# One-hots for an edge selection written as 2-byte marks and widened on a second engine, with six tiles selected in two chunks of five

## The chip, the cores and the metric

The kernel runs on one core of a Trainium2 chip. The metric is the device time of one execution in microseconds (us). Before the change the runs shown have a median of 3418.08 us, and the execution that was profiled took 3413.38 us. A core has five engines that run their own instruction streams and meet at semaphores: TensorE (PE, matrix products), VectorE (DVE), ScalarE (ACT), GpSimd (POOL, here the engine that starts row gathers) and SyncE (SP, here a queue of plain DMAs).

## The reference

One graph-attention layer over 12500 nodes and 400000 edges, the edges sorted by destination:

```python
h = jnp.maximum(_layernorm(x, axis=-1), 0.0)
xl = jnp.einsum('ni,nio->no', h, hetero_w[node_type]) + hetero_b[node_type]
ete = _lrelu(edge_type_emb[edge_type])
eae = _lrelu(edge_attr @ edge_attr_w)
alpha = _lrelu(jnp.concatenate([xl[dst], xl[src], ete, eae], axis=-1) @ att_w)
amax = jax.ops.segment_max(alpha, dst, num_segments=N)
alpha = jnp.exp(alpha - amax[dst])
denom = jax.ops.segment_sum(alpha, dst, num_segments=N)
alpha = alpha / (denom[dst] + 1e-16)
msg = jnp.concatenate([xl[src], eae], axis=-1) @ lin_w * alpha
out = x + jax.ops.segment_sum(msg, dst, num_segments=N)
```

## The kernel before

A prologue builds a table with one row of 34 numbers for each node (its contribution to messages and its two attention scores) and stores it in DRAM. The edges then go by in 125 chunks. A chunk has 25 tiles of 128 edges, one edge of a tile on each partition. The loop body is five chunks long (`u` = 0 to 4, each with its own buffers) and runs 25 times; the last pass is written out for most engines.

For each edge the table row of its source node is needed. It comes in one of two ways. **20 of the 25 tiles are gathered**: POOL issues one indirect DMA per tile (`gather_chunk`, line 598), two chunks ahead. **Five tiles are selected** (`TS = 5`): DVE compares a broadcast list of codes with constants and so writes one-hot matrices in a 4-byte format (`select_onehots`, lines 1150 and 1152, seven compares for `sel_a`, the first three tiles, and seven for `sel_b`, the last two); PE multiplies them with the table, which lies in SBUF in seven groups and two parts (`select`, 14 products at line 834 and one at 836), into the one PSUM bank `ps_sel`; DVE takes the row out of the bank (`take`, line 1164). There is a single bank, so `select` number j waits for `take` number j-1 (`sel_read`), and `take` j waits for `select` j (`sel_mm`).

Everything else of a chunk: PE computes destination scores in seven steps (`dst_scores`, line 848, read by DVE in `picks`, line 1172), the edge attributes (`attr_product`, 858), messages (`messages`, 869) and sign counts (`count_signs`, 878). DVE adds gathered rows to the messages (line 1241), forms the scores and a running maximum, hands `args` to ACT (1263), and scans the weighted messages in two halves (`scan_half`, 1220). ACT takes the exponential (728), spreads it into `keep` (735), which the first scan waits for, copies the sums into rows (741), starts their store (744), and writes the sign matrices for the next chunk (`make_signs`, 718 and 720).

The order on each engine is written out by hand. DVE's pass for chunk c works on chunk c's sums and on the selection and scores of chunk c+1, whose products PE runs at the same time: `take` 0 stands after `select_rest` for c+1, `take` 1 between the two scans, `take` 2 behind the attribute activation, `select_first` (for c+2) behind that, and then `take` 3 and `take` 4. On PE the five `select`s of a chunk stand between the steps of `dst_scores`.

At the end a fix-up joins runs of edges that cross partitions: SP waits for all row stores and loads the last row of each partition back into `tails`, DVE and PE work on it, POOL gathers one row (`own`, 613) and scatters one (616). Then POOL gathers 98 blocks of rows for the nodes, in eight groups of 19, 17, 17 and five times 9 (`last_in_buf`, line 639), and DVE finishes each group when its gathers have landed (lines 1468 to 1480): marks of a node's last block in `is_node` and `is_last`, a product with them (1472), two reductions (1474, 1475), a reciprocal, a product and a sum, after which SP stores the group.

Of the kernel before, what the change touches and what calls it, by code (L numbers as in the profile page):

```python
# [14 lines left out]
P = 128  # L15
# [22 lines left out]
TS = 5  # L38
TS_A = 3
SEL = CHUNKS * TS  # L40
GATHERED = T - TS
TURNS = tuple(GATHERED * k // 5 for k in range(6))
# [24 lines left out]
def gnn_kernel(nc, x, meta, dst_rows, dst_tmajor, type_tmajor, sel_src, row_edges, row_last, edge_attr_t, node_type,  # L67
# [20 lines left out]
    with ctx:  # L88
# [99 lines left out]
        compared = node_buf[:, 2 * TG * P:2 * TG * P + (EPP + 1) // 2].bitcast(bf16)[:, 0:EPP]  # L188
        eae_s = in_node_buf(0, [2, TG * P // 2], G * F_EDGE)
        eae = in_node_buf(TG * P, [2, TG * P // 2], G * F_EDGE)  # L190
        dstc = [sb(f"dstc{u}", [P, T + 1]) for u in range(U)]
# [29 lines left out]
        def part_of(k, g):  # L221
            return parts[:, k, g, :].rearrange("p (f n) -> p f n", n=GN)

        last_in_buf = [(buf.rearrange("p (n j f) -> p n j f", j=BLOCK, f=RW), n) for buf, n in (
            *((b.bitcast(fp32)[:, 0:9 * BLOCK * RW], 9)
              for b in (*(buf[:] for buf in hib_sb), onehot[:].rearrange("p t e -> p (t e)"))),
# [3 lines left out]
        is_node = hm[0][:].rearrange("p a b -> p (a b)")[:, 0:NPP * (BLOCK + 1)].rearrange("p (n j) -> p n j", j=BLOCK + 1)  # L230
        is_last = hm[1][:].rearrange("p a b -> p (a b)")[:, 0:NPP * BLOCK].rearrange("p (n j) -> p n j", j=BLOCK)
# [16 lines left out]
        tails = sb("tails", [P, RW])  # L248
# [31 lines left out]
        ps_hmT = [ps_attr, ps_pick]  # L280

# [61 lines left out]
        eae_scaled = sem("eae_scaled")  # L343
        eae_ready = sem("eae_ready")
# [13 lines left out]
        tails_in = sem("tails_in")  # L358
# [31 lines left out]
        out_ready = sem("out_ready")  # L390
        out_done = sem("out_done")
# [6 lines left out]
        def selected(i, u):  # L398

            return (i * U + u) * TS  # L400
# [12 lines left out]
        def _(sp):  # L413
# [95 lines left out]

            for u in range(U):  # L510
                sp.wait_ge(stored[u], 16 * ITERS + 1)
            flag = is_unsorted(sp)
            sp.wait_ge(sel_mm, count(CHUNKS * TS))
            sp.dma_start(x_end[:], x).then_inc(x_end_in, 16)
            with sp.If(flag < 1):
                sp.dma_start(tails[:], rows_pm[:, EPP - 1, :]).then_inc(tails_in, 16)
                sp.wait_ge(tails_in, 16)
# [17 lines left out]
        def _(pool):  # L535
# [50 lines left out]
            def gather_chunk(i, u, first):  # L586
# [6 lines left out]
                for k, (phase, reached) in enumerate(phases):  # L593
                    if not first:
                        pool.wait_ge(phase, reached)
                        pool.sem_inc(gather_turns, 1)
                    for t in range(TURNS[k], TURNS[k + 1]):
                        nc.gpsimd.indirect_dma_start(  # L598
                            gath[u][:, t, :], None, table_dram,
                            bass.IndirectOffsetOnAxis(ap=meta_sb[u][:, t:t + 1], axis=0)).then_inc(gathered[u], 16)  # L600

            for u in range(U):
                gather_chunk(0, u, u < AHEAD)
            with pool.Fori(1, ITERS) as i:
                for u in range(U):
                    gather_chunk(i, u, False)

            for u in range(U):
                pool.wait_ge(stored[u], 16 * ITERS + 1)
            flag = is_unsorted(pool)  # L610
            with pool.If(flag < 1):
                pool.wait_ge(head_idx_ready, 1)
# [32 lines left out]
        def _(act):  # L645
            start_at_one(act, rows_sums, *stored)
# [65 lines left out]

            def make_signs(c, u):
# [10 lines left out]
            def chunk(i, u, final):  # L724
                c = i * U + u

                act.wait_ge(args_ready, c + 1)
# [16 lines left out]
                act.dma_start(rows_pm[:, ds(c * T, T), :], rows[u][:]).then_inc(stored[u], 16)  # L744
                if not final:
# [3 lines left out]
            make_signs(0, 0)  # L749
            with act.Fori(0, ITERS - 1) as i:  # L750
# [21 lines left out]
        def _(pe):  # L772
# [51 lines left out]
            def select(c, j):  # L824

                if j == 0:
                    pe.wait_ge(sel_a_ready, c + 1)
                elif j == TS_A:
                    pe.wait_ge(sel_b_ready, c + 1)
                rows_of, slots_of, at = (sel_a, slot_a, j) if j < TS_A else (sel_b, slot_b, j - TS_A)  # L830
                pe.wait_ge(sel_read, count(c * TS + j))
# [52 lines left out]
            with pe.Fori(0, ITERS) as i:  # L884
                for u in range(U):
                    c = i * U + u
                    dst_scores(c, 0)
                    select(c, 0)
                    attr_product(i, u)
                    dst_scores(c, 1)  # L890
                    select(c, 1)
                    dst_scores(c, 2)
                    dst_scores(c, 3)
                    select(c, 2)
                    dst_scores(c, 4)
                    messages(c)
                    select(c, 3)
                    dst_scores(c, 5)
                    dst_scores(c, 6)
                    select(c, 4)  # L900
                    count_signs(c)

            pe.wait_ge(falls_ready, 1)
            pe.wait_ge(sel_read, count(CHUNKS * TS))
            nc.tensor.matmul(ps_misc[:, 0, 0:1], before_me[:], falls[:, 0:1], start=True, stop=True).then_inc(
                falls_mm, 1)
# [7 lines left out]
            with pe.If(flag < 1):  # L914
                pe.wait_ge(tails_in, 16)
# [5 lines left out]
                nc.tensor.matmul(ps_misc[:, 0, 2 * P:2 * P + VW], wtailT[:], tails[:, 0:VW], start=True,  # L921
# [14 lines left out]
        def _(dve):  # L936
# [208 lines left out]
            def select_onehots(i, u, tiles, rows_of, slots_of, ready):  # L1145
# [3 lines left out]
                for g in range(NG):  # L1149
                    v.tensor_scalar(rows_of[:, g, :, 0:P], code_sb[u][:, edges], part_group[:, g:g + 1], None,  # L1150
                                    ALU.is_equal)
                v.tensor_scalar(slots_of[0:GN, :, 0:P], slot_sb[u][:, edges], part[0:GN, :], None,  # L1152
                                ALU.is_equal).then_inc(ready, 1)

            def select_first(i, u):
                select_onehots(i, u, slice(0, TS_A), sel_a, slot_a, sel_a_ready)

            def select_rest(i, u):
                select_onehots(i, u, slice(TS_A, TS), sel_b, slot_b, sel_b_ready)
# [65 lines left out]
            def chunk(i, u, at, final):  # L1225
# [4 lines left out]
                last_front = isinstance(i, int) and c + 2 >= CHUNKS  # L1230

# [5 lines left out]
                dve.wait_ge(gathered[u], (i + 1) * (16 * GATHERED))  # L1237
                dve.wait_ge(msg_mm, count(c + 1))
                dve.wait_ge(sel_read, count(selected(i, u) + TS))
# [4 lines left out]
                if not final:  # L1244
                    select_rest(*after)
# [31 lines left out]
                if not final:  # L1277
                    picks(front, 2)
                    attr_act(front)
                    take(*after, 2)  # L1280
                    picks(front, 3)
                    if not last_front:
                        select_first(*later)
                    picks(front, 4)
                    take(*after, 3)
# [5 lines left out]
                    take(*after, 4)  # L1291
# [4 lines left out]
            select_first(0, 0)  # L1296
# [14 lines left out]
            select_rest(0, 0)  # L1311
# [72 lines left out]


            flag = is_unsorted(dve)
            with dve.If(flag < 1):
                joined_step = stage(join_step)
                dve.wait_ge(tails_in, 16)
                v.tensor_copy(mtail[:], tails[:, VW:VW + 1].broadcast_to([P, P])).then_inc(head_idx_ready, 1)  # L1390
# [70 lines left out]
            finished = stage(last_step)  # L1461

            finished(v.memset(is_node, 0.0))
            dve.wait_ge(x_end_in, 16)
            for k, (buf, w) in enumerate(last_in_buf):
# [3 lines left out]
                                         node_id[:, n].unsqueeze(2).broadcast_to([P, w, BLOCK]), ALU.is_equal))  # L1469
                finished(v.tensor_tensor(is_last[:, n, :], is_node[:, n, 0:BLOCK], is_node[:, n, 1:BLOCK + 1],  # L1470
# [59 lines left out]
```

## Time and profile before

| | |
|---|---|
| median of the runs shown | 3418.08 us |
| the profiled execution | 3413.38 us |
| its span, first to last instruction | 3411.6 us |
| PE busy | 3067.4 us (90%) |
| DVE busy | 2951.0 us (86%) |
| POOL busy | 2495.9 us (73%) |
| ACT busy | 900.4 us (26%) |
| mean granted TensorE clock | 0.954 |

Busy shares are means over a prologue of some 150 us, the loop of about 3090 us and an end of some 170 us. POOL's share leaves out the fixed time between two DMA issues, which the profile counts as idle for "issue". Matmuls overlap, so the time from the start of one group to the start of the next says more than their durations; the same holds for short DVE instructions in a row.

### The profile page before, as it was taken

What the parts mean: (1) busy time and instruction counts of PE and PEld (TensorE: products, weight loads), DVE (VectorE), ACT (ScalarE), POOL (GpSimd) and SP (SyncE); (2) the same over time, 40 slices, a digit from 0 to 9 for tenths busy, and PEclk for the clock granted to TensorE, in tenths of its full rate; (3) what the DMA queues carried; (4) which work ended last, traced back from release to release, by engine and by line L of the source; (5) the groups of instructions that cost most, each with busy time, mean ns of one, the idle gap of its engine ahead of it and who ended that gap; (6) DMA issues with size and microseconds to landing.
All of it is one profiled execution on the core that took longest, in us unless ns stands there. A gap on an engine that the chain in (4) does not pass through costs nothing.

```text
span 3411.6 us, 66571 instructions
## 1 busy us (share of the span) xinstructions
PE 3067.4 (90%) x21488; PEld 2610.0 (77%) x21488; DVE 2951.0 (86%) x7241; ACT 900.4 (26%) x2094; POOL 2495.9 (73%) x2629
## 2 busy tenths in 40 slices
PE   7799999999999999999999999999999999999900
PEld 6688888878878888888888888888887887887700
DVE  6799999889889888988989889888988988998835
ACT  3223232223222232222323223232222222222200
POOL 2577777777777777777777777777777777777656
PEclk6799999999999999999999999999999999999955
DMA  3433333333333333333333333333333333336322
GB/s 119 117 73 91 72 91 72 91 72 86 77 72 91 72 88 76 79 85 72 91 72 83 80 72 91 72 88 78 76 89 72 91 72 73 91 72 153 74 74 73
DMA packets 186011, 284.37 MB, mean 83 GB/s; under 512 B 73954, under 2 KB 140986, under 8 KB 185212
## 3 DMA queue, kind: packets, MB, share of 16 engines
q1 hardware_dynamic: 76796, 165.55, 16.1%
q0 software_dynamic: 84768, 52.50, 13.0%
q10 hardware_dynamic: 24288, 64.79, 5.3%
q14 instruction: 131, 1.07, 0.1%
q8 instruction: 28, 0.46, 0.1%
HBM read 210.13 MB, written 72.48 MB: 83 GB/s over the span
## 4 chain that ended last, share of the span: by engine, by line
DVE 28%; PE 27%; POOL 23%; issue 17%; DMA 4%; DVEq 0%; POOLq 0%; ACT 0%; SPq 0%; ACTq 0%
POOL gath L598 20%; PE ps_misc L834 19%; DVE sel_a L1150 10%; DMA gath<-table_dram,meta 4%; DVE sel_b L1150 4%; DVE gath L1164 3%; PE ps_pick L848 3%; DVE dscore L1172 3%; DVE slot_a L1152 1%; PE ps_misc L836 1%; DVE ps_msg L1241 1%; PE ps_misc L804 1%; POOL hib L639 1%; DVE ps_misc L1211 1%; PE ps_attr L858 1%
## 5 line engine op out<-in xcount | busy, mean ns | idle before, releaser
L598 POOL DMA_INDIRECT gath<-table_dram,meta x2500 | 2364.3, 946 | 831.8 <-issue 733.3
L834 PE MATMUL ps_misc<-parts,sel_a 128*128 128x462 f32 x5250 | 1219.0, 383 | 94.3 <-DVE gath L1164 94.1
L834 PEld LDWEIGHTS ps_misc<-parts,sel_a 128*128 128x128 f32 x5250 | 973.9, 191 | 220.6 <-DVE gath L1164 120.4
L834 PE MATMUL ps_misc<-parts,sel_b 128*128 128x462 f32 x3500 | 806.5, 381 | 28.4 <-DVE gath L1164 25.0
L834 PEld LDWEIGHTS ps_misc<-parts,sel_b 128*128 128x128 f32 x3500 | 644.9, 189 | 117.8 <-DVE gath L1164 43.6
L848 PE MATMUL ps_pick<-s_dst,onehot 122*128 122x128 bf16 x9375 | 652.4, 220 | 29.6 <-DVE s_dst L1304 14.2
L848 PEld LDWEIGHTS ps_pick<-s_dst,onehot 122*128 122x128 bf16 x9375 | 540.0, 98 | 172.9 <-issue 126.2
L1172 DVE TENSOR_REDUCE dscore<-ps_pick 128x4 f32<-128x512 f32 x875 | 521.5, 618 | 1.2 <-PE ps_pick L848 1.1
L1164 DVE TENSOR_REDUCE gath<-ps_misc 128x33 f32<-128x462 f32 x625 | 391.9, 627 | 142.3 <-PE ps_misc L836 142.3
L728 ACT ACTIVATE wts<-args 128x50 f32<-128x50 f32 x125 | 30.8, 246 | 1680.5 <-DVE args L1263 1680.5
L1150 DVE TENSOR_SCALAR sel_a<-dst_f,part_group 128x384 fp32r<-128x384 f16 x875 | 465.4, 604 | 0.0
L741 ACT COPY rows<-sums 128x825 f32<-128x825 f32 x125 | 231.2, 1849 | 500.0 <-DVE sums L1220 500.0
L1220 DVE TENSOR_TENSOR_SCAN sums<-keep,ps_misc 128x416 f32<-128x416 f32 x250 | 261.9, 1048 | 9.3 <-ACT keep L735 0.3
L1150 DVE TENSOR_SCALAR sel_b<-dst_f,part_group 128x256 fp32r<-128x256 f16 x875 | 266.3, 375 | 0.0
L718 ACT ACTIVATE hi_f<-half,hic 128x128 bf16<-128x128 f32 x625 | 243.5, 390 | 82.3 <-ACT rows L741 77.1
L1185 DVE TENSOR_SCALAR onehot<-hib,row_code 122x3200 bf16<-122x3200 bf16 x125 | 232.1, 1857 | 0.0
L720 ACT ACTIVATE hi_f<-half,loc 128x98 bf16<-128x98 f32 x625 | 226.2, 362 | 0.0
L1241 DVE TENSOR_TENSOR ps_msg<-gath,ps_msg 128x495 f32<-128x495 f32 x250 | 135.8, 589 | 87.0 <-DMA gath<-table_dram,meta 86.4
L869 PE MATMUL ps_msg<-msg_w,node_buf 80*128 80x165 f32 x1250 | 202.4, 309 | 0.0
L869 PEld LDWEIGHTS ps_msg<-msg_w,node_buf 80*128 80x128 f32 x1250 | 177.7, 190 | 0.0
L1211 DVE TENSOR_TENSOR ps_misc<-ps_msg,wts 128x240 f32<-128x240 f32 x500 | 159.2, 364 | 0.2 <-ACT wts L728 0.2
L858 PE MATMUL ps_attr<-attr,attr_w 80*80 80x320 f32 x500 | 155.1, 432 | 0.0
(239 smaller groups left out, 1933.5 us busy)
## 6 DMA issues: line engine op xcount, KB each, us to landing
hib<-digit_dram SPq DMA_DIRECT2D x125, 612.5 KB
rows_dram<-rows ACTq DMA_DIRECT2D x125, 437.5 KB, 5.0
gath<-table_dram,meta POOLq DMA_INDIRECT x2500
attr<-edge_attr_t_in SPq DMA_DIRECT2D x125, 200.0 KB
dst_f<-sel_code_dram SPq DMA_DIRECT2D x125, 160.0 KB
hib<-digit_dram SPq DMA_DIRECT2D x250, 50.0 KB
rows_dram<-no_rows ACTq DMA_DIRECT2D x1, 8575.0 KB, 44.5
hib<-digit_dram SPq DMA_DIRECT2D x250, 25.0 KB
```

The source lines that it names most:

```text
L598: nc.gpsimd.indirect_dma_start(gath[u][:, t, :], None, table_dram, bass.IndirectOffsetOnAxis(ap=meta_sb[u][:, t:t + 1], axis=0)).then_inc( ...
L718: nc.scalar.activation(sign_hi[:, t, :], half128[:], ACT.Sign, bias=hic[u][:, t:t + 1], scale=-1.0)
L720: last = nc.scalar.activation(sign_lo[:, t, :], half128[:, 0:NPP], ACT.Sign, bias=loc[u][:, t:t + 1], scale=-1.0)
L741: nc.scalar.copy(rows[u][:, :, 0:VW], sums[:, :, 1:T + 1].rearrange("p f t -> p t f")).then_inc(rows_sums, 1)
L834: nc.tensor.matmul(ps_sel, rows_of[:, g, at, 0:P], parts[:, k, g, :], start=(g == 0 and k == 0), stop=False)
L848: last = nc.tensor.matmul(ps_pick[:, g % 2, j * LO:(j + 1) * LO], onehot[0:KD, t, 0:P], s_dst[0:KD, k, :], start=(k == 0), stop=(k == 2))
L869: last = nc.tensor.matmul(ps_msg[:, g // 3, g % 3 * G * VW:(g % 3 + 1) * G * VW], eae_flat[:, g * P:(g + 1) * P], msg_w[:], start=True, st ...
L1150: v.tensor_scalar(rows_of[:, g, :, 0:P], code_sb[u][:, edges], part_group[:, g:g + 1], None, ALU.is_equal)
L1164: v.tensor_reduce(gath[u][:, T - 1 - j, 0:VW], ps_sel.rearrange("p (f n) -> p f n", n=GN), AX.X, ALU.max).then_inc(sel_read, 1)
L1172: v.tensor_reduce(dscore[:, tiles], ps_pick[:, g % 2, 0:n * LO].rearrange("p (t m) -> p t m", m=LO), AX.X, ALU.max).then_inc(picked, 1)
L1185: v.tensor_scalar(onehot[0:KD, :, 0:P], hib_sb[HIB_OF[u]][0:KD, :], row_code[0:KD, :], None, ALU.is_equal).then_inc(onehot_ready, 1)
L1220: return v.tensor_tensor_scan(sums[:, f0:f1, :].rearrange("p f t -> p (f t)"), keep[:, f0:f1, :].rearrange("p f t -> p (f t)"), terms[:, 0 ...
```

## The change

The selection's one-hots are made in two steps. DVE's compares for chunks after the first now write contiguous bf16 marks into one shared buffer `marks` (`select_marks`, seven compares of 384 or 256 numbers), and ACT copies the marks, widened to the 4-byte format, into `sel_a` (`widen_first`, 7x384 numbers) and `sel_b` (`widen_rest`, 7x256 or 7x384). Two new semaphores order this: `marks_ready` (DVE to ACT) and `marks_widened` (ACT to PE, and to DVE before the buffer is written again). The small one-hots of slots stay with DVE.

The number of selected tiles follows `TS_OF = (5, 6, 5, 6, 5)`: chunks with `u` = 1 and 3 select six tiles and gather 19. A pass of the loop selects 27 tiles instead of 25 and gathers 98 instead of 100; over the kernel POOL issues 2450 gathers instead of 2500.

In the end, the last rows of the partitions are read where they still lie in SBUF (`row_tails`) and the load of `tails` is gone; POOL's gather of `own` no longer waits for DVE; clearing `is_node` is moved ahead; `is_last`, a copy of `node_id`, the reciprocals and the averages lie in PSUM; the last group of nine nodes is split in six and three; and `count_falls` and the load of `x_end` stand a little earlier.

```diff
-TS = 5
+TS_OF = (5, 6, 5, 6, 5)
+TS = max(TS_OF)
 TS_A = 3
-GATHERED = T - TS
-TURNS = tuple(GATHERED * k // 5 for k in range(6))
...
+            (hib_sb[0][:].bitcast(fp32)[:, 6 * BLOCK * RW:9 * BLOCK * RW], 3),
+            (hib_sb[0][:].bitcast(fp32)[:, 0:6 * BLOCK * RW], 6),
...
+        is_last = [in_bank(ps_msg, 0, BLOCK * last_at[k], w, BLOCK) for k, (_, w) in enumerate(last_in_buf)]
+        inverse = ps_msg[:, 1, 0:NPP]
+        node_of = ps_msg[:, 1, NPP:2 * NPP]
+        averaged = ps_pick[:].rearrange("p a b -> p (a b)")
+        row_tails = rows[U - 1][:, T - 1, :]
...
+            def widen_rest(i, u):
+                c = i * U + u
+                before = (i, u - 1) if u else (i - 1, U - 1)
+                n = TS_OF[u] - TS_A
+                act.wait_ge(marks_ready, 2 * c)
+                act.wait_ge(sel_mm, count(selected(*before) + TS_OF[before[1]]))
+                nc.scalar.copy(sel_b[:, :, 0:n, 0:P],
+                               marks[:, :, 0:n * P].rearrange("p g (t e) -> p g t e", e=P)).then_inc(marks_widened, 1)
...
+            def select_marks(i, u, tiles, widened):
+                edges = slice(tiles.start * P, tiles.stop * P)
+                dve.wait_ge(code_in[u], (i + 1) * 32)
+                dve.wait_ge(marks_widened, widened)
+                for g in range(NG):
+                    last = v.tensor_scalar(marks[:, g, 0:edges.stop - edges.start], code_sb[u][:, edges],
+                                           part_group[:, g:g + 1], None, ALU.is_equal)
+                last.then_inc(marks_ready, 1)
...
                 if not final:
                     picks(front, 2)
                     attr_act(front)
-                    take(*after, 2)
+                    if takes > 2:
+                        take(*after, 2)
                     picks(front, 3)
                     if not last_front:
                         select_first(*later)
+                    if takes > 5:
+                        take(*after, 3)
                     picks(front, 4)
-                    take(*after, 3)
+                    if takes > 3:
+                        take(*after, takes - 2)
```

On PE, in a chunk with `u` = 1, from its second `select` to the step after its third; before:

```order
L834 MATMUL ps_misc<-parts,sel_a 128x462 x14
L836 MATMUL ps_misc<-slot_pen,slot_a 128x462
L842 REGISTER_ALU
L848 MATMUL ps_pick<-s_dst,onehot 128x128 x12
L842 REGISTER_ALU
L848 MATMUL ps_pick<-s_dst,onehot 128x128 x12
L831 REGISTER_ALU
L834 MATMUL ps_misc<-parts,sel_a 128x462 x14
L836 MATMUL ps_misc<-slot_pen,slot_a 128x462
L842 REGISTER_ALU
L848 MATMUL ps_pick<-s_dst,onehot 128x128 x12
```

The same place now, on to the fourth `select`, which uses the first tile of `sel_b`:

```order
L884 MATMUL ps_misc<-parts,sel_a 128x462 x14
L886 MATMUL ps_misc<-slot_pen,slot_a 128x462
L892 REGISTER_ALU
L898 MATMUL ps_pick<-s_dst,onehot 128x128 x12
L881 REGISTER_ALU
L884 MATMUL ps_misc<-parts,sel_a 128x462 x14
L886 MATMUL ps_misc<-slot_pen,slot_a 128x462
L892 REGISTER_ALU
L898 MATMUL ps_pick<-s_dst,onehot 128x128 x12
L879 REGISTER_ALU
L881 REGISTER_ALU
L884 MATMUL ps_misc<-parts,sel_b 128x462 x14
```

Where two score steps stood between the second and the third `select`, one stands now, and one between the third and the fourth; chunks with five tiles keep the old order.

On ACT, one chunk from the exponential (728 before, 772 now) to the first sign matrix (718, 757); before:

```order
L728 ACTIVATE wts<-args 128x50
L731 COPY rows<-mrun 128x25
L732 COPY rows<-dstc 128x25
L735 COPY keep<-wts 128x33x25
L709 REGISTER_ALU
L711 ACTIVATE node_buf<-ps_attr 80x640
L741 COPY rows<-sums 128x25x33
L744 ISA
L744 DMA rows_dram<-rows 128x875
L718 ACTIVATE hi_f<-half,hic 128x128
```

And now, the two widening copies being the lines named CAST:

```order
L749 CAST sel_b<-node_buf 128x7x2x128
L772 ACTIVATE wts<-args 128x50
L775 COPY rows<-mrun 128x25
L776 COPY rows<-dstc 128x25
L779 COPY keep<-wts 128x33x25
L729 REGISTER_ALU
L731 ACTIVATE node_buf<-ps_attr 80x640
L785 COPY rows<-sums 128x25x33
...
L739 CAST sel_a<-node_buf 128x21x128
L757 ACTIVATE hi_f<-half,hic 128x128
```

One widening stands ahead of the exponential and one ahead of the sign matrices.

## Rows read from the trace of the kernel before

**Rows 1.** One line's instructions, L598: ns min/median/max, first and last start in us.
```profile
L598 POOL DMA_INDIRECT gath<-table_dram,meta x2500: 940/944/3264, 107.2 to 3232.2; - x193
```

**Rows 2.** The same view of L1243, which DVE runs once in a chunk.
```profile
L1243 DVE COPY mrun<-mrun x125: 148/149/154, 151.5 to 3237.9; 128x1 f32<-128x1 f32 x125
```

**Rows 3.** Waits of the whole span: engine line waited for: us in total, times, longest us.
```profile
DVE ps_msg L1241 <- DMA gath<-table_dram,meta: 86.4, 71, 6.6
...
DVE sign_sums L1179 <- issue: 57.7, 23, 2.7
```

**Rows 4.** Window of one chunk: us, busy us by engine (instructions), PEclk, DMA.
```profile
212.00:235.70 23.70, 23.41 (x172) 20.14 (x171) 22.36 (x57) 6.33 (x16) 17.91 (x20) 1.00 0.34 81
```

**Rows 5.** Page, costliest groups: line engine op, shapes xcount | busy us, mean ns | idle.
```profile
L1150 DVE TENSOR_SCALAR sel_a<-dst_f,part_group 128x384 fp32r<-128x384 f16 x875 | 465.4, 604 | 0.0
L1185 DVE TENSOR_SCALAR onehot<-hib,row_code 122x3200 bf16<-122x3200 bf16 x125 | 232.1, 1857 | 0.0
```

**Rows 6.** Timeline of PE, one chunk: start us, us, instructions [idle before <-releaser].
```profile
229.82 1.52 PE L848 MATMUL ps_pick<-s_dst,onehot 122*128 122x128 bf16 x24
231.14 3.19 PE L834 MATMUL ps_misc<-parts,sel_a 128*128 128x462 f32 x14
...
234.39 0.84 PE L848 MATMUL ps_pick<-s_dst,onehot 122*128 122x128 bf16 x12
...
239.69 1.27 PE L848 MATMUL ps_pick<-s_dst,onehot 122*128 122x128 bf16 x15
241.17 3.22 PE L834 MATMUL ps_misc<-parts,sel_b 128*128 128x462 f32 x14 [0.20 <-DVE gath L1164]
```

**Rows 7.** Timeline of DVE in the same chunk.
```profile
222.73 2.17 DVE L1150 TENSOR_SCALAR sel_b<-dst_f,part_group 128x256 fp32r<-128x256 f16 x7
...
229.37 1.02 DVE L1220 TENSOR_TENSOR_SCAN sums<-keep,ps_misc 128x416 f32<-128x416 f32 x1
230.31 0.61 DVE L1164 TENSOR_REDUCE gath<-ps_misc 128x33 f32<-128x462 f32 x1
...
234.59 0.64 DVE L1164 TENSOR_REDUCE gath<-ps_misc 128x33 f32<-128x462 f32 x1 [0.52 <-PE ps_misc L836]
...
235.74 3.72 DVE L1150 TENSOR_SCALAR sel_a<-dst_f,part_group 128x384 fp32r<-128x384 f16 x7
```

**Rows 8.** Timeline of ACT in the same chunk.
```profile
226.86 0.25 ACT L728 ACTIVATE wts<-args 128x50 f32<-128x50 f32 x1 [12.39 <-DVE args L1263]
...
227.23 0.89 ACT L735 COPY keep<-wts 128x825 f32<-128x825 f32 x1
```

**Rows 9.** Window with the sign matrices' tile alone: us, ACT busy us (instructions), PEclk, DMA.
```profile
235.50:238.50 3.00, 2.91 (x10) 1.00 0.96 254
```

**Rows 10.** Groups of ACT by form: line engine op, shapes xcount | busy us, mean ns | idle.
```profile
L698 ACT CAST hib<-dst_f 128x3125 bf16<-128x3125 int32 x1 | 2.8, 2792 | 0.0
L741 ACT COPY rows<-sums 128x825 f32<-128x825 f32 x125 | 231.2, 1849 | 500.0 <-DVE sums L1220 500.0
```

**Rows 11.** Timeline of the end, several engines (SPq: a DMA started by SP).
```profile
3248.84 0.35 SPq L514 DMA_DIRECT2D x_end<-x_in  x1
...
3256.02 0.94 POOL L613 DMA_INDIRECT own<-rows_dram,head_idx  x1 [22.86 <-DVE mtail L1390]
...
3265.70 0.98 POOL L639 DMA_INDIRECT node_buf<-rows_dram,pos  x1 [2.36 <-issue]
...
3291.66 3.42 DVE L1472 TENSOR_TENSOR node_buf<-node_buf,hm 128x3135 f32<-128x3135 f32 x1
3292.01 3.89 POOL L639 DMA_INDIRECT hi_f<-rows_dram,pos  x1 [0.31 <-issue]
...
3400.23 0.95 POOL L639 DMA_INDIRECT hib<-rows_dram,pos  x1 [0.30 <-issue]
...
3402.82 0.23 DVE L1468 TENSOR_TENSOR hm<-hib,node_id 128x45 f32<-128x45 f32 x1 [5.36 <-DMA hib<-rows_dram,pos]
...
3408.93 0.46 DVE L1480 TENSOR_TENSOR h<-h,x_end 128x288 f32<-128x288 f32 x1
```

More of the change, by code:

```diff
@@ L35, with turns @@
 SIGNS_AFTER = PICKS - 1
-TS = 5
+TS_OF = (5, 6, 5, 6, 5)
+TS = max(TS_OF)
 TS_A = 3
+TS_LAST = 5
 SEL = CHUNKS * TS
-GATHERED = T - TS
-TURNS = tuple(GATHERED * k // 5 for k in range(6))
+SELECTED = ITERS * sum(TS_OF) - TS_OF[-1] + TS_LAST
+def turns(n):
+    return tuple(n * k // 5 for k in range(6))
 HIB_OF = (0, 1, 2, 3, 1)
@@ L398, in selected @@
         def selected(i, u):
-            return (i * U + u) * TS
+            return i * sum(TS_OF) + sum(TS_OF[0:u])
         def start_at_one(eng, *sems):
@@ L725, in chunk @@
                 c = i * U + u
+                after = (i if u < U - 1 else i + 1, (u + 1) % U)
+                later = (i if u < U - 2 else i + 1, (u + 2) % U)
+                last_front = isinstance(i, int) and c + 2 >= CHUNKS
+                if not last_front or (not final and TS_LAST > TS_A):
+                    widen_rest(*after)
                 act.wait_ge(args_ready, c + 1)
@@ L744, in chunk @@
                 act.dma_start(rows_pm[:, ds(c * T, T), :], rows[u][:]).then_inc(stored[u], 16)
+                if not last_front:
+                    widen_first(*later)
                 if not final:
@@ new lines, in chunk @@
+            def chunk(i, u, final):
+                c = i * U + u
+                tiles = TS_LAST if final else TS_OF[u]
+                dst_scores(c, 0)
+                select(i, u, 0)
+                attr_product(i, u)
+                dst_scores(c, 1)
+                select(i, u, 1)
+                dst_scores(c, 2)
+                if tiles > 5:
+                    select(i, u, 2)
+                dst_scores(c, 3)
+                if 2 < tiles <= 5:
+                    select(i, u, 2)
+                if tiles > 5:
+                    select(i, u, 3)
+                dst_scores(c, 4)
+                messages(c)
+                if tiles > 3:
+                    select(i, u, tiles - 2)
+                dst_scores(c, 5)
+                dst_scores(c, 6)
+                if tiles > 3:
+                    select(i, u, tiles - 1)
+                if final:
+                    count_falls()
+                count_signs(c)
@@ L907, in _ @@
+            with pe.Fori(0, ITERS - 1) as i:
+                for u in range(U):
+                    chunk(i, u, False)
+            for u in range(U):
+                chunk(ITERS - 1, u, u == U - 1)
             pe.wait_ge(sign_parts_ready, 1)
@@ L1230, in chunk @@
                 last_front = isinstance(i, int) and c + 2 >= CHUNKS
+                takes = TS_LAST if isinstance(i, int) and c + 2 == CHUNKS else TS_OF[after[1]]
                 if final:
@@ L1244, in chunk @@
                 if not final:
-                    select_rest(*after)
+                    if takes > TS_A:
+                        select_rest(*after)
                     take(*after, 0)
@@ L1290, in chunk @@
                     penalties(after[1], at)
-                    take(*after, 4)
+                    if takes > 3:
+                        take(*after, takes - 1)
             for n in range(4):
```

143 lines of the change are left out of this document (79 added, 64 removed).

## The prediction

> **What bounds the kernel now.** I read the instructions of the gather's line first. POOL issues 2500 gathers, the first at 107.2 us and the last at 3232.2 us, each 940 to 944 ns long [rows 1]: one every 3125.0 / 2499 = 1.25 us, so 20 of them take 25.0 us a chunk. The chunk's own rhythm is the copy of `mrun`, which DVE runs once in a chunk: (3237.9 - 151.5) / 124 = 24.89 us [rows 2], or 124.4 us for a pass of five. The two agree, so over the whole loop POOL sets the pace. The waits say so as well: DVE waits 71 times for gathered rows, 86.4 us in all [rows 3].
>
> Next I asked how far behind POOL the others are. Early in the loop the gathers are still ahead, and one chunk takes 23.70 us there, with PE busy for 23.41, DVE for 22.36 and ACT for only 6.33 at the full granted clock of 1.00 [rows 4]. Once in a pass DVE stands still before its first instruction, with nothing that the profile can name: 23 listed times, 57.7 us, so 2.5 us each [rows 3]. A pass without gathers would take 5 x 23.70 + 2.5 = 121.0 us, only 3.4 us less than now. PE is the second bound, close behind the first, and this change takes two gathers from POOL and gives two selections to PE.
>
> **POOL after the change.** A pass gathers 98 tiles: 98 x 1.25 = 122.5 us, a possible gain of 1.9 us on 124.4.
>
> **PE, chunks with five tiles.** A `select` costs PE 234.39 - 231.14 = 3.25 us from its start to that of the next step [rows 6]. One wait inside the chunk comes from the old compares. Before the last `select`, PE has 15 score products, which need 15/24 of the 1.32 us (229.82 to 231.14) that 24 take, 0.82 us; but the `select` starts 1.48 us after them (239.69 to 241.17), behind the `take` that stands in DVE's queue after 3.72 us of compares for `sel_a` [rows 6, 7]. If marks are short, this `take` is only held by its own `select`: it starts 0.20 us after it (234.59 against 234.39) and lasts 0.64 [rows 6, 7]; with 0.05 to the next `select` that is 0.89 us, 0.59 less. A five-tile chunk then takes 23.70 - 0.59 = 23.11 us.
>
> How short marks are, the trace does not show. DVE's nearest 2-byte compare with 2-byte output takes 1857 ns for 3200 numbers, 0.58 ns each, and would give 0.22 us for 384; the present compares come every 3.72 / 7 = 0.53 us [rows 5, 7]. I take the lower end, since input and output are of that row's width. It is also where marks lie beside PE's products and cost nothing; at the upper end the relief of 0.59 is gone (a rival below).
>
> **PE, chunks with six tiles.** Two chunks of a pass get one `select` more, 3.25 us, and their order loses cover. Today 24 score products stand between the second and third `select`; now 12 do (0.66 us), and 12 more after the third. There is one bank, so the third `select` needs the second `take`, which stands on DVE between the scans and ends at 230.31 + 0.61 = 230.92, while PE is done with the second `select` at 229.82 [rows 6, 7]. So the third starts at about 230.97, 1.15 after the second, ends at 234.22; the fourth follows 0.89 later and ends at 238.36. The same work up to there, without the extra `select`, ends at 234.39 now. That is 3.97 more, 0.72 of it bare waiting: 23.11 + 3.97 = 27.08 us.
>
> **The sum in the loop.** 3 x 23.11 + 2 x 27.08 + 2.5 = 126.0 us a pass, more than POOL's 122.5: PE, with DVE's `take`s in between, becomes the bound, and POOL starts to wait. For 124 chunks (24 passes and four chunks of 100.4 us): 24 x 126.0 + 100.4 = 3124.4, against 3086.4 now. That is +38.0 us.
>
> **Widening on ACT** is costed at nothing. Its price is bounded by two rows. ACT's plain cast of 3125 numbers takes 2792 ns, 0.89 ns each; its copy of 825 numbers into a transposed place takes 1849 ns, 2.24 each [rows 10]. For 2688 numbers that is 2.4 or 6.0 us, for 1792 1.6 or 4.0. The widened rows are runs of 128 in order, so I take the cast. What hides it: ACT idles 12.39 us before the exponential [rows 8]. The rest compares start at 222.73, seven marks would end by 224.3 (they took 2.17 us, to 224.9), and a cast of 2.4 us ends at 226.7; the exponential starts at 226.86 now, and 0.6 us earlier if DVE's gain is passed on [rows 7, 8]. The next in line is `keep`: it ends at 227.23 + 0.89 = 228.12, and the scan that needs it starts at 229.37 [rows 7, 8]. So about 0.6 us of slack remain. The other cast stands ahead of the sign matrices, whose making keeps ACT busy for 2.91 us [rows 9]: marks from 235.74 end at 237.3, plus 2.4 and 2.9 gives 242.6, and PE wants them after its last `select`, 241.17 + 3.25 - 0.59 = 243.8 [rows 6, 7]. Slack 1.2 us.
>
> **The end.** POOL's load of `own` starts at 3256.02 after 22.86 us of waiting for `mtail`; the stores are known to have landed when SP goes on at 3248.84 [rows 11]. Without the load of `tails` it can start there: -7.2 us. The 98 node gathers start over 3400.23 - 3265.70 = 134.5 us, where 97 x 1.25 = 121.3 would do. One that starts during DVE's product of `node_buf` with `hm` (3.42 us) lasts 3.89 us [rows 11]. With one factor in PSUM this should cease: between 0 and -13.3, and I take -13.3, as plain gathers beside the loop's compares keep their 944 ns. The last group of nine takes 3402.82 to 3408.93 + 0.46, 6.6 us [rows 11]; three nodes, with six still in work when they land, about 4.5: -2.1. Sum -22.5 us (-9 to -23).
>
> **Forecast A.** The profiled run took 3413.4 us, 4.7 under the median of 3418.1. 3413.4 + 38.0 - 22.5 = 3428.9, so 3429 us: 0.3% longer. A measurement of this kernel tells about 2% from no change, so this counts as the same. With the `take`s up to 0.7 us earlier or later in each six-tile chunk (35 us over the loop) and the end's bounds, its own range is 3395 to 3460.
>
> **Rivals.**
> B, POOL stays the bound. The waits of PE and DVE's stop of 2.5 us vanish behind each other, 5 x 23.11 + 2 x 3.25 = 122.1 us, and the pass is 122.5: 24.8 x 122.5 = 3038, -48.4, with the end 3342 us. For it: the relief also moves DVE's `take`s earlier. Against: the exchange between `select` and `take` through one bank is no slack of DVE's, it is latency. Chance 0.05; for a partial gain, 3342 to 3395, 0.12.
>
> C, on the other side: widening at 2.24 ns. The sign matrices come at 237.3 + 6.0 + 2.9 = 246.2, 2.4 us after PE's `select`s end, in every chunk: 24.8 x 5 x 2.4 = +298, with the end and A's loop 3727 us at the least. It decides from about 3.7 us for a cast of 2688 numbers, and each tenth beyond costs 12 us. For it: output of 4 bytes a number and a three-level shape. Against: the cast's row. Chance 0.06.
>
> D: marks stop POOL. The two runs of marks in a chunk last 14 x 0.22 = 3.1 us or so; gathers that stand still for them make the pass 122.5 + 15.5 = 138 us, 3422 for the loop, 3727 in all. It decides from (126.0 - 122.5) / 5 = 0.7 us lost in a chunk. Against: the gathers' median of 944 ns beside compares of 2-byte output as well [rows 1, 5]. Chance 0.04. The Trainium skill ("SBUF — State Buffer", section "Who interferes with whom") has a rule of this kind: a VectorE instruction in a two-port mode, which `tensor_scalar` can enter, holds ports that GpSimd needs too, and the other one blocks fully. The long gather beside the product of two SBUF operands looks like such a block; in the loop the even pace of 1.25 us beside 14 selection compares a chunk leaves no room for one [rows 1, 11].
>
> E: marks are no faster than 0.53 us. No relief, and signs at 239.5 + 2.4 + 2.9 = 244.8, 0.4 late: 3 x 24.1 + 2 x 28.1 + 2.5 = 131.0 a pass, 3249 for the loop, +162: 3553 us. Chance 0.04.
>
> **How the numbers follow.** A 0.69, partial gain 0.12, B 0.05, C 0.06, D 0.04, E 0.04. The range should leave out no more than 2 in 10: from 3365, the middle of the partial gains, to 3475, a little above A's own range for casts just past their slack; it leaves out B, half of the partial gains and most of C, D and E. Faster by over 2% is under 3350: B, 0.05. Slower by over 2% is over 3486: most of C, D and E, 0.11. The same: 0.84.
>
> **What the profile after would show.** Right, if POOL's gathers no longer follow each other at 1.25 us through the loop but wait for DVE's `picks`; if DVE's wait for gathers goes; if PE's chunks take 23.1 and 27.1 us with the wait before the third `select` of a six-tile chunk; if a mark of 384 takes about 0.22 us and a cast of 2688 about 2.4 us; if `own` starts with the last store and no node gather exceeds 1 us. Wrong, if PE waits for sign matrices (C), gathers stretch (D), DVE still waits for gathers at 122.5 us a pass (B), or the six-tile chunk costs less than one `select` more.

## The result, and the profile after

The changed kernel takes 3528.5 us (median of four runs, 3526.4 to 3531.9), before 3417.9: a ratio of 1.033 (95% interval 1.031 to 1.035). One of the four executions before the change took 10804 us and is left out of the ratio. The changed kernel is 3.3% slower, where 0.3% and at most 3475 us were forecast. The profiled execution has a span of 3527.1 us.

First the same views as before the change: the gathers' line, the copy of `mrun` (one line's instructions: ns min/median/max, first and last start), and three waits of the whole span (us in total, times, longest us).

```profile
L617 POOL DMA_INDIRECT gath<-table_dram,meta x2450: 939/946/3534, 108.1 to 3351.2; - x189
```

```profile
L1334 DVE COPY mrun<-mrun x125: 147/149/152, 149.8 to 3374.9; 128x1 f32<-128x1 f32 x125
```

```profile
POOL gath L617 <- DVE dscore L1258: 204.5, 159, 5.6
...
PE ps_pick L898 <- issue: 64.9, 23, 3.1
DVE sign_sums L1265 <- issue: 60.3, 23, 2.8
```

The loop takes (3374.9 - 149.8) / 24.8 = 130.0 us a pass, where [rows 2] gave 124.4 and 126.0 were forecast. The end is shorter: from the last `mrun` to the end of the span 3527.1 - 3374.9 = 152.2 us, before 3411.6 - 3237.9 = 173.7. So the loop lost 139 us and the end gained 21.5. DVE's wait for gathered rows [rows 3] is no longer among the waits; POOL now waits for DVE, 204.5 us. DVE's stop at the start of its pass is as before. But PE has a stop of its own, 23 times, 2.8 us each, with nothing that the profile names as its cause.

This is a timeline of PE in the middle of the loop. L928 are the sign counts that end a chunk, L898 the score products that begin the next.

```profile
1525.18 0.40 PE L928 MATMUL ps_pick<-hi_f 128*128 128x98 bf16 x5
...
1548.27 0.40 PE L928 MATMUL ps_pick<-hi_f 128*128 128x98 bf16 x5
1551.34 0.84 PE L898 MATMUL ps_pick<-s_dst,onehot 122*128 122x128 bf16 x12 [2.66 <-issue]
...
1574.20 0.40 PE L928 MATMUL ps_pick<-hi_f 128*128 128x98 bf16 x5
...
1581.66 3.20 PE L884 MATMUL ps_misc<-parts,sel_a 128*128 128x462 f32 x14 [1.42 <-DVE gath L1250]
...
1587.27 3.24 PE L884 MATMUL ps_misc<-parts,sel_a 128*128 128x462 f32 x14 [1.51 <-DVE gath L1250]
...
1604.18 0.40 PE L928 MATMUL ps_pick<-hi_f 128*128 128x98 bf16 x5
...
1627.27 0.40 PE L928 MATMUL ps_pick<-hi_f 128*128 128x98 bf16 x5
```

A five-tile chunk takes 23.09 us (1525.18 to 1548.27, and 1604.18 to 1627.27). The next, 25.93, starts with the stop; PE's loop begins anew there. Then comes the six-tile chunk in which DVE starts its pass anew, 29.98. Over 23 passes (the first and the last left out) the starts of L928 give, in the order `u` = 1, 2, 3, 4, 0 of the chunk whose products PE runs, 30.21, 23.10, 27.09, 23.10 and 26.63: together 130.1.

The pieces on which the forecast stood were measured too. Marks on DVE, casts on ACT (groups by form), and the gathers of the end (first and last start of nineteen and of thirty-six, POOL's load of `own`, and the last addition):

```profile
1527.16 1.45 DVE L1233 TENSOR_SCALAR node_buf<-dst_f,part_group 128x256 bf16<-128x256 f16 x7
1540.16 1.86 DVE L1233 TENSOR_SCALAR node_buf<-dst_f,part_group 128x384 bf16<-128x384 f16 x7
```

```profile
L739 ACT CAST sel_a<-node_buf 128x2688 fp32r<-128x2688 bf16 x124 | 302.6, 2441 | 395.4 <-DVE node_buf L1233 380.2 <-issue 15.2
L749 ACT CAST sel_b<-node_buf 128x1792 fp32r<-128x1792 bf16 x74 | 125.2, 1692 | 528.2 <-DVE node_buf L1233 528.2
```

```profile
3385.77 0.94 POOL L633 DMA_INDIRECT own<-rows_dram,head_idx  x1 [33.65 <-DMA rows_dram<-rows]
```

```profile
L659 POOL DMA_INDIRECT hib<-rows_dram,pos x36: 942/947/950, 3473.7 to 3517.5; - x36
L659 POOL DMA_INDIRECT node_buf<-rows_dram,pos x19: 942/947/981, 3396.1 to 3418.7; - x19
```

```profile
3524.87 0.26 DVE L1582 TENSOR_TENSOR h<-ps_pick,x_end 128x96 f32<-128x96 f32 x1
```

Seven marks of 384 take 1.86 us where seven compares took 3.72 [rows 7], 0.27 us each; a cast of 2688 numbers takes 2441 ns. In the end `own` starts 10.9 us after the last `mrun` (18.1 before), and the 98 node gathers start over 121.4 us (134.5 before).

Where does PE's stop come from? The page's part on DMA queues has one line that changed by a factor of eight. First the kernel before, then the changed one (queue, kind: packets, MB, share):

```profile
q8 instruction: 28, 0.46, 0.1%
```

```profile
q8 instruction: 224, 3.67, 0.4%
```

These are blocks of 16 KB of program. That they are PE's is read from their times: in the trace of the changed kernel they come at every pass, nine of them from 1455.1 to 1584.8, and before the change they come along the first pass and then not again, except in two passes around 2230 to 2461 us. So before, PE's loop body stayed in its instruction memory, and after the change it is brought anew in every pass. In the stop shown above, from 1548.67 to 1551.34 us, one of these blocks is on its way, from 1548.56 for 1.03 us; what fills the rest of the stop the trace does not show. Counted between two loop branches in the trace, the body has 1774 instructions before and 1846 after: 30 products and as many weight loads more for two `select`s, and twelve for waits and their registers.

### The profile page after: what moved, and what is told of

Read it like the earlier page. It is cut to its first block, busy times and chain, and to the rows that moved or that the text cites. A ratio compares the mean times of both kernels' runs of the same rounds, so it can differ in the third digit from the quotient of the medians.

```text
span 3527.1 us, 69260 instructions
## 1 busy us (share of the span) xinstructions
PE 3190.6 (90%) x22238; PEld 2745.7 (78%) x22238; DVE 2716.4 (77%) x7301; ACT 1433.7 (41%) x2342; POOL 2453.0 (70%) x2579
## 3 DMA queue, kind: packets, MB, share of 16 engines
q8 instruction: 224, 3.67, 0.4%
## 4 chain that ended last, share of the span: by engine, by line
PE 75%; DVE 10%; issue 9%; POOL 3%; ACT 2%; DVEq 0%; DMA 0%; ACTq 0%; POOLq 0%
PE ps_misc L884 50%; PE ps_pick L898 11%; PE ps_msg L919 5%; PE ps_misc L886 3%; DVE gath L1250 2%; PE ps_attr L908 2%; DVE node_buf L1233 2%; PE ps_misc L851 1%; POOL hib L659 1%; DVE ps_msg L1332 1%; ACT L749 1%; ACT keep L779 1%; ACT sel_b L749 1%; PE ps_pick L928 1%; POOL node_buf L659 1%
## 5 line engine op out<-in xcount | busy, mean ns | idle before, releaser
L617 POOL DMA_INDIRECT gath<-table_dram,meta x2450 | 2333.0, 952 | 980.5 <-issue 690.1
L884 PE MATMUL ps_misc<-parts,sel_b 128*128 128x462 f32 x4200 | 965.8, 380 | 4.8 <-DVE gath L1250 2.4
L1250 DVE TENSOR_REDUCE gath<-ps_misc 128x33 f32<-128x462 f32 x675 | 428.2, 634 | 573.7 <-PE ps_misc L886 573.2
L884 PEld LDWEIGHTS ps_misc<-parts,sel_b 128*128 128x128 f32 x4200 | 772.5, 189 | 98.6 <-DVE gath L1250 13.1
L898 PE MATMUL ps_pick<-s_dst,onehot 122*128 122x128 bf16 x9375 | 643.8, 220 | 79.2 <-issue 64.9
L898 PEld LDWEIGHTS ps_pick<-s_dst,onehot 122*128 122x128 bf16 x9375 | 542.7, 98 | 217.1 <-issue 201.6
L749 ACT CAST sel_b<-node_buf 128x1792 fp32r<-128x1792 bf16 (+1 forms) x124 | 247.3, 1994 | 654.8 <-DVE node_buf L1233 654.5
L739 ACT CAST sel_a<-node_buf 128x2688 fp32r<-128x2688 bf16 x124 | 302.6, 2441 | 395.4 <-DVE node_buf L1233 380.2
L1233 DVE TENSOR_SCALAR node_buf<-dst_f,part_group 128x384 bf16<-128x384 f16 x1736 | 425.3, 319 | 0.0
L886 PE MATMUL ps_misc<-slot_pen,slot_a 128*128 128x462 f32 x375 | 139.1, 371 | 0.0
```

What stands on the lines that cost most here:

```text
L617: nc.gpsimd.indirect_dma_start(gath[u][:, t, :], None, table_dram, bass.IndirectOffsetOnAxis(ap=meta_sb[u][:, t:t + 1], axis=0)).then_inc( ...
L739: nc.scalar.copy(sel_a[:, :, :, 0:P], marks.rearrange("p g (t e) -> p g t e", e=P)).then_inc(marks_widened, 1)
L749: nc.scalar.copy(sel_b[:, :, 0:n, 0:P], marks[:, :, 0:n * P].rearrange("p g (t e) -> p g t e", e=P)).then_inc(marks_widened, 1)
L884: nc.tensor.matmul(ps_sel, rows_of[:, g, at, 0:P], parts[:, k, g, :], start=(g == 0 and k == 0), stop=False)
L886: nc.tensor.matmul(ps_sel, slots_of[:, at, 0:P], slot_pen[:].rearrange("p f n -> p (f n)"), start=False, stop=True).then_inc(sel_mm, 1)
L898: last = nc.tensor.matmul(ps_pick[:, g % 2, j * LO:(j + 1) * LO], onehot[0:KD, t, 0:P], s_dst[0:KD, k, :], start=(k == 0), stop=(k == 2))
```

## Experiments

Three theories of the stop: **F**, the body now touches nine blocks instead of eight, because of its place; **L**, it is too long, wherever it lies; **W**, it is the last pass, now written out behind the loop. Later a fourth, **M**: marks, casts and their semaphores make it.

**The body moved by 80 instructions.** In PE's prologue:

```diff
+            for _ in range(40):
+                nc.tensor.matmul(ps_pick[:, 0, 0:1], zeros[:, 0:P], zeros[:, 0:1], start=True, stop=True)
             transposes(0)
```

> The changed kernel with 40 more products of one column (80 instructions) on PE once, in its prologue, and nothing else. Theory F (fetch by place): PE's loop body no longer stays in its instruction memory, because with its length and its place it touches nine blocks of code of 16 KB; the trace of the changed kernel has 224 blocks on PE's instruction queue and PE stands still about 2.7 us at each loop start, sometimes 5. Moved by 80 instructions the same body touches eight blocks: under 50 fetches, the stop of 2.7 us at the pass boundary gone, a pass of 126.3 us instead of 130, total 3528 - 24 x 3.6 = 3440. Theory L (length alone): the body of some 1846 instructions is too long wherever it lies: still 8 or 9 blocks a pass, 3528 to 3531. Theory W (the last pass written out behind the loop): as L, no change.

Measured: 3528.1 us (3523.6 to 3532.2), 224 blocks, the same stop. F falls, at least for this shift and this length.

**The loop over all 25 passes.**

```diff
-            with pe.Fori(0, ITERS - 1) as i:
+            with pe.Fori(0, ITERS) as i:
                 for u in range(U):
                     chunk(i, u, False)
-            for u in range(U):
-                chunk(ITERS - 1, u, u == U - 1)
+            count_falls()
```

> The changed kernel with PE's loop over all 25 passes, as before the change, and not 24 with the last pass written out behind it. Theory W (writing the last pass out makes PE fetch its code anew at each loop start): stop of 2.7 us gone, about 3440. Theories F and L (length of the body, alone or with its place): the place and length of the body are the same, the stop stays, 3528 plus one more stop of 2.7, within 0.3%.

Measured: 3532.0 us (3523.7 to 3540.6), 226 blocks, 24 stops. W falls.

**Five tiles everywhere, and one chunk of six.**

```diff
-TS_OF = (5, 6, 5, 6, 5)
+TS_OF = (5, 5, 5, 5, 5)
```

> The changed kernel with five selected tiles in every chunk: marks, widening and the new end stay, POOL gathers 100 tiles a pass as before. Theories F and L: PE's body is about as short as before (some 1790 instructions), PE's instruction queue is quiet, PE chunks of 23.1 us, POOL the bound at 125.0 us a pass: 3086 for the loop, the end 21 us shorter than before, 3395. Theory W: PE still stops 2.7 us a pass, but POOL hides it: the same time, with over 200 blocks on PE's instruction queue. If marks and widening themselves cost PE or POOL time, it is above 3410.

Measured: 3405.2 us (3404.3 to 3406.4), ratio 0.997 (0.995 to 0.998). That is 10 us more than expected, and PE's queue still has 224 blocks: with 1784 instructions the body does not stay. The loop is POOL-bound, (3250.9 - 149.4) / 24.8 = 125.1 us a pass, so the stop is mostly hidden.

```diff
-TS_OF = (5, 6, 5, 6, 5)
+TS_OF = (5, 5, 6, 5, 5)
```

> The changed kernel with six tiles in the chunk with u = 2 alone (5, 5, 6, 5, 5): 99 gathers a pass, 26 selections. My sum by chunks: PE 4 x 23.1 + 27.1 + 2.8 for DVE's stop = 122.3 us a pass, POOL 99 x 1.25 = 123.75, so POOL is the bound: 24.8 x 123.75 = 3069, with the shorter end 3378. If PE's body (some 1815 instructions) is fetched anew in each pass, 2.7 to 3.6 us more on PE, 125.0 to 125.9 a pass: 3409 to 3431.

Measured: 3409.9 us (3406.7 to 3414.2), 224 blocks with 1815 instructions. It is the second expectation: the chunks are 24.94, 26.98, 23.11, 23.10 and 27.04 us, 125.2 a pass, over POOL's 123.75.

**Ten instructions more in the kernel before.** This separates L from M: no mark, no cast, five tiles, and a body as long as in the kernel with five tiles and marks.

```diff
+                if g == 0:
+                    nc.tensor.matmul(ps_pick[:, 0, 0:1], onehot[0:KD, 0, 0:P], s_dst[0:KD, 0, 0:1],
+                                     start=True, stop=True)
                 for t in range(g * PICK_T, min(T, (g + 1) * PICK_T)):
```

> The kernel before with one product of one column more in front of the first score product of each chunk: five products, ten instructions more in PE's loop body (1784 instead of 1774 in the trace, as many as in the kernel with five tiles), overwritten by the product behind it. Theory L (the length of PE's body decides whether its code stays in its instruction memory, and the limit lies between 1774 and 1784): blocks on PE's instruction queue rise from 28 to over 200, PE stops 2.7 us at its loop start in nearly each pass; POOL's slack of about 3 us a pass hides most of it, so 3416 to 3440. Rival M (marks, widening or their semaphores make the stop): the queue stays near 28 blocks, no stop, 3416 to 3420.

Measured: 3415.9 us, ratio 0.9995 (0.999 to 1.0005). The page's queue line and PE's wait at the loop start (before the change, the second of these lines read 3.8 us, 2 times):

```profile
q8 instruction: 226, 3.70, 0.5%
```

```profile
PE ps_pick L846 <- issue: 34.0, 24, 1.7
```

Ten instructions turn 28 blocks into 226 and bring a stop in each pass, here 1.4 us; the time does not move, since POOL sets the pace and PE has the slack. L holds, M is not needed. One rival is left at this limit: the ten instructions also move the end of the body, and no run separates its length from the number of blocks that it touches there.

**The changed kernel with a shorter body.**

```diff
-                    for k in range(3):
+                    for k in range(3 if g < 4 else 2):
...
-                                                start=(k == 0), stop=(k == 2))
+                                                start=(k == 0), stop=(k == (2 if g < 4 else 1)))
```

> The changed kernel without the third part of the score products in the last nine tiles of a chunk (45 products, 90 instructions a pass left out; the low bits of these scores are left out with them): some 1756 instructions in PE's loop body, 27 selections a pass as in the change. Theory L: PE's instruction queue quiet, stop of 2.7 to 5 us gone (3.4 on average), and 45 x 0.055 = 2.5 us less work: a pass of 130.0 - 3.4 - 2.5 = 124.1 us, total 3528 - 24.8 x 5.9 = 3382. Rival M: the stop stays, 127.5 us a pass, 3466.

Measured: 3444.5 us (3440.8 to 3453.4), 84 us less than the change.

```profile
q8 instruction: 61, 1.00, 0.1%
```

```profile
PE ps_pick L898 <- issue: 21.1, 5, 4.5
```

With 1756 instructions and 27 selections a pass the stop is gone in 18 of 23 passes. The chunk that had it takes 22.87 us in these. Two sizes were wrong. The products left out saved 1.3 us a pass, not 2.5: 0.22 in a five-tile chunk, since there the last `select` waits 0.15 us for a `take` instead, and 0.31 and 0.38 in the two with six. And five passes are 6 us longer: the body is brought anew there, at a stop of 4.2 us. Why a body of 1756 or 1774 instructions is lost now and then stays open.

**Six-tile chunks off the start of DVE's pass.**

```diff
-TS_OF = (5, 6, 5, 6, 5)
+TS_OF = (5, 5, 6, 6, 5)
```

> The changed kernel with the six-tile chunks at u = 2 and 3 instead of u = 1 and 3, so that none of them falls on the chunk in which DVE starts its pass anew. By the chunks of the change (30.2 us there, 27.1 elsewhere) and of the kernel with one six-tile chunk (24.9 for a five-tile chunk there, 27.0 and 23.1 elsewhere): 24.9 + 27.1 + 27.1 + 23.1 + 26.5 = 128.7 us a pass instead of 130.0, total 3528 - 24.8 x 1.3 = 3496. If the place of DVE's stop makes no difference: 3528.

Measured: 3514.1 us (3511.9 to 3517.1). Chunks of 24.93, 26.99, 26.99, 23.11 and 27.33 us, 129.4 a pass. The first four came as expected; DVE's stop costs a five-tile chunk 1.8 us and a six-tile one 3.1. But the chunk with PE's stop got dearer, 27.33 instead of 26.63, so only 14 us of 32 remain. The stop itself is no longer (62.5 us in 23 times); the clock is lower behind it. In 20 of the 23 chunks that start with it, the granted clock falls to 0.50 for a stretch, and they take 27.3 to 27.8 us; the other three take 25.7 to 25.9. In the change it falls in six (below).

**PE's old waits.** ACT's casts increment the two semaphores that PE waited for before, which takes ten instructions out of PE's body; for this the small compare of slots moves ahead of the marks (five tiles).

```diff
...
                 dve.wait_ge(freed, widened)
+                select_slots(u, tiles, slots_of)
                 for g in range(NG):
...
```

> Five selected tiles in every chunk, marks and the new end as in the change, but ACT's widening itself increments the two semaphores that PE waited for before, and DVE compares the slots ahead of the marks: PE's loop body has 1774 instructions again, ten fewer than in the kernel with five tiles and separate semaphores (3405 us). Theory L: the queue is quiet again, no stop, POOL is the bound without breaks: about 5 to 8 us less, 3397 to 3400. Rival M: over 200 blocks, stop as before, 3405.

Measured: 3632.6 us, a ratio of 1.063, which neither theory had foreseen. PE's queue did go down, to 107 blocks. But 246 gathers of 2500 lasted more than 1 us, 245 us over their usual time in all. The two runs of marks in each of 124 chunks make 248, and 244 of the 246 lie over a mark: nearly every run holds one gather. This is rival D of the prediction, in a kernel that was not forecast. Two runs separate its cause: the first puts the marks back ahead of the slots and keeps the merged semaphores, the second is the kernel with five tiles where only the slots are moved ahead.

> As the kernel with five tiles and PE's waits as before (3632 us, where 246 gathers lasted about 2 us), but with the marks ahead of the slots' compare again, which then starts ACT's widening. Theory Q (a slow compare right ahead of the seven marks lets them queue up and run without a gap, and POOL's gather is held for the whole run): gathers 944 ns again, fewer than 150 over 1000 ns, with an excess under 20 us in all; and by theory L PE's body of 1774 instructions stays in its memory: 3397 to 3402. Rival S (the merged semaphores, not the order, hold the gathers): again some 246 long gathers, about 3630.

> The kernel with five tiles (3405 us) with the slots' compare ahead of the marks and nothing else changed, all semaphores and their increments as there. Theory Q: some 246 gathers of about 2 us, 245 us lost on POOL, about 3630 us. Rival S: gathers as in the kernel with five tiles (109 over 1000 ns, excess 13 us), about 3405.

Measured: 3403.5 us (3401.1 to 3404.7) with the marks first, 103 gathers over 1 us and 13 us in excess; 3634.4 us (two runs) with the slots first, 246 gathers and 241 us. It is the order. The timelines of DVE and POOL, first the kernel with the slots ahead, then the kernel with five tiles, which has the marks ahead:

```profile
517.06 0.33 DVE L1224 TENSOR_SCALAR slot_b<-hi_f,part 14x256 fp32r<-14x256 f16 x1
517.32 1.45 DVE L1234 TENSOR_SCALAR node_buf<-dst_f,part_group 128x256 bf16<-128x256 f16 x7
517.46 2.01 POOL L617 DMA_INDIRECT gath<-table_dram,meta  x1 [0.30 <-issue]
```

```profile
518.67 1.45 DVE L1233 TENSOR_SCALAR node_buf<-dst_f,part_group 128x256 bf16<-128x256 f16 x7
519.32 1.04 POOL L617 DMA_INDIRECT gath<-table_dram,meta  x1 [0.30 <-issue]
520.04 0.43 DVE L1224 TENSOR_SCALAR slot_b<-hi_f,part 14x256 fp32r<-14x256 f16 x1
```

The marks take the same 1.45 us; in the first the gather lasts until they are through, in the second it is 0.1 us longer than usual. That marks queue up behind a slow compare and then leave no gap is a guess that fits; the runs show the order, not the reason. With the marks first and 1774 instructions PE's queue has 116 blocks, and PE still stops in 11 passes. The merged waits were worth 1.7 us, not 5 to 8, and the two intervals (0.995 to 0.998 both) do not tell that from nothing.

**The new end alone.** Five tiles, and compares write the 4-byte one-hots as before, without marks and casts:

```diff
-TS_OF = (5, 6, 5, 6, 5)
+TS_OF = (5, 5, 5, 5, 5)
...
-                select_marks(i, u, tiles, 2 * (i * U + u))
+                select_rows(i, u, tiles, sel_a)
                 select_slots(u, tiles, slot_a, sel_a_ready)
...
```

> The kernel before with the new end alone: compares write the 4-byte one-hots themselves, no marks, no widening, five tiles in every chunk, PE's waits and loop body as before (1774 instructions). The loop as before, the end 21 us shorter: 3396. If the marks had given the loop anything, this would be slower than the kernel with five tiles and marks (3405); I expect it 5 to 10 us faster, since no mark stretches a gather and PE does not stop.

Measured: 3396.5 us (3395.2 to 3399.4), ratio 0.994 (0.993 to 0.996). It is the fastest of these kernels: the change's end without its loop. PE was expected not to stop; it stops in seven passes, with 80 blocks, though its body has 1774 instructions as before the change. POOL sets the pace, and the time came as expected.

## Why the prediction was wrong

The range ended at 3475 us, and the kernel took 3528.5. By the steps:

- **POOL stops being the bound: right.** 98 x 1.25 would be 122.5 us a pass; POOL waited for DVE instead.
- **Five-tile chunks, 23.11 us: right**, 23.09 to 23.10. The wait behind the old compares went as reckoned.
- **Six-tile chunks, 27.08 us: right**, 27.09 where no loop starts.
- **DVE's stop, 2.5 us a pass: undersized.** It falls on a six-tile chunk, which it lengthens by 30.21 - 27.09 = 3.1 us. Its stop holds one `take`, and the next `select`s wait 1.42 and 1.51 us one after the other, with a single bank and one score step between them. 0.6 x 23 = 14 us.
- **The start of PE's loop, nothing: this step failed.** "A pass without gathers would take 5 x 23.70 + 2.5" counted the stop that the trace of before showed, DVE's, and the sum for the new pass, 3 x 23.11 + 2 x 27.08 + 2.5, has no term for PE's own. I did not ask what the change does to the length of PE's program. The chunk with PE's stop takes 26.63 - 23.10 = 3.53 us more; 3.53 x 23 = 81 us.
- **Marks, 0.22 us: they take 0.27 and it was enough. Casts, 2.4 us beside other work: right**, 2441 ns.
- **The end, -22.5: right**, -21.5; `own` 7.2 us earlier as reckoned, node gathers 13.1 us shorter (13.3 reckoned).

With 81 and 14 us more, 3429 becomes 3524. Another 6 us lie in the last pass, which PE runs written out: by the starts of L928 it takes 131.8 us, where 126.0 were reckoned for every pass; against that the first `mrun` comes 1.7 us earlier than before.

PE's 3.5 us are the 2.8 of the stop, 0.2 around it, and 0.5 on average for a loss of clock behind it in some passes. In 17 of the 23 chunks that start with the stop the granted clock stays at 1.00, the level of 2.4 GHz, and they take 25.8 to 26.3 us. In the other six it falls to 0.50, the level of 1.2 GHz, and they take 27.4 to 29.1. This is the one of 29.1; then two windows, its stretch and one behind the stop shown above (us; busy us of PE, weight loads, DVE, ACT, POOL; granted clock; DMA):

```profile
1681.07 1.46 PE L898 MATMUL ps_pick<-s_dst,onehot 122*128 122x128 bf16 x12 [3.10 <-issue]
1682.29 5.32 PE L884 MATMUL ps_misc<-parts,sel_a 128*128 128x462 f32 x14
```

```profile
1680.10:1686.90 6.80, 5.83 (x24) 5.25 (x25) 1.16 (x6) 1.69 (x1) 5.04 (x6) 0.50 0.12 15
1551.00:1560.00 9.00, 8.66 (x58) 7.43 (x58) 5.37 (x23) 3.54 (x6) 4.96 (x7) 1.00 0.11 13
```

PE had stood for 3.10 us, and fourteen products then took 5.32 us instead of 3.2. Stops of 3.1 us also stand among the 17, and one of 2.5 among the six, so the stop's length alone does not decide; what does stays open.

The Trainium skill ("Runtime: NRT & Kernel Launch", section "Instruction fetch mechanics") says that an engine's code comes in blocks of 16 KiB, that a taken branch to a target outside the two blocks held costs a fetch, and that PE's memory holds 2048 instructions. The blocks agree with the trace (224 in 3.67 MB). The two blocks do not: before the change PE's branch back over 1774 instructions brought no block in most passes. Nor does the count: 1784 instructions, as the trace counts them, are brought anew in every pass, while 1774 stayed in all but two passes of the kernel before and were lost more often in three others (80, 107 and 116 blocks). With the 2048 of the Trainium skill the forecast would have stood; a count of the body, 1774 before and 1846 after, beside the 28 blocks of the queue's line would have raised the question.

Of the rivals none was it. D showed only in the order that the change does not have: in the changed kernel some 140 gathers are 0.1 us longer. These cost under 17 us on POOL, which is no longer the bound. The rule of the Trainium skill that I weighed ("SBUF — State Buffer", section "Who interferes with whom") speaks of one VectorE instruction that blocks GpSimd as long as it lasts; with the slots first a gather was held 1.07 us, longer than any one of the seven marks that take 1.45 us together. So the trace agrees with the kind of block and not with its length, and no run shows which mode or port the marks used.

## What to carry to other kernels

Before adding instructions to a long hardware loop, look at the instruction queues on the profile's page: few blocks for a loop of many passes mean that the body stays in the engine's memory, and then its length is a resource that can run out, here with ten instructions on top of 1774. When a change moves work from one engine to the next tightest, list what each pass costs that engine besides its products: its own loop start, and the stops of its partner, which cost more where less work stands between two exchanges through one bank: DVE's stop cost a five-tile chunk 1.8 us and a six-tile one 3.1. And take a bundle of edits apart: here the end alone gave all the gain there was, 0.6%.

## What the runs showed that I had not expected

- A loop body of PE of 1774 instructions stayed in place for all but two passes of the kernel before (28 blocks), and one of 1784 for none (226 blocks). Three other kernels with 1774 lost it in 7 to 11 passes (80 to 116 blocks). The stop at the loop's start was 2.8 us on average in the change, 1.4 us in the kernel before with ten instructions more, and 4.2 us in the five passes that the shorter body lost.
- Seven short 2-byte compares in a row held a gather of POOL for up to their whole run (2.01 us instead of 0.94) when a slow compare stood right ahead of them, and by 0.1 us at most in the typical case when it stood behind: 241 to 245 us a kernel from the order of two steps.
- After a stop of PE of 2.5 to 3.1 us the granted clock fell to 0.50 for a stretch in 6 of 23 passes of the change and in 20 of 23 with the six-tile chunks moved. Such a pass lost 1.8 to 2.1 us more than one whose clock stayed at 1.00, so a stop can cost more than it lasts.
